# Attention and gated MLP in one program: the odd pair sums of attention's last unit go to VectorE, and the third accumulating DMA is issued behind pair 5 instead of pair 4

## The reference

```python
h = _layernorm(x, axis=-1) * (1 + ca) + sa
x = x + ga * _L0_attn_ref(h, Wq, Wk, Wv, Wo, bo)
h = _layernorm(x, axis=-1) * (1 + cb) + sb
x = x + gb * _L0_ffn_ref(h, w_gate, w_up, w_down)
```

```python
att = jnp.einsum('bhgqd,bhkd->bhgqk', q, k) / scale
att = jax.nn.softmax(att, axis=-1)
y = jnp.einsum('bhgqk,bhkd->bhgqd', att, v)
y = y.transpose(0, 3, 1, 2, 4).reshape(b, t, e)
return y @ Wo.T + bo
```

## Time and profile before

| | before |
|---|---|
| median of 3 runs | 3463.37 us (3461.37 to 3470.88) |
| profiled execution, span from the first to the last instruction | 3460.0 us |
| TensorE busy (matmuls) | 3409.4 us, 99% |
| VectorE, ScalarE, GpSimd busy | 65%, 46%, 47% |
| mean granted clock of TensorE | 0.995 |
| attention, last unit's end | 1988 us |

### The profile page before, as it was taken

One profiled execution on the slowest core, in us unless ns is written; L12 is line 12 of the kernel. 1 busy time (PEld: TensorE's weight loads), 2 busy tenths in 40 slices (PEclk: granted clock), 3 DMA queues, 4 the chain that ended last, 5 costly groups with the idle time before them and its releaser, 6 DMA issues.

```text
span 3460.0 us, 45394 instructions
## 1 busy us (share of the span) xinstructions
PE 3409.4 (99%) x17032; PEld 2290.5 (66%) x17032; DVE 2248.4 (65%) x3760; ACT 1597.7 (46%) x3008; POOL 1635.8 (47%) x728
## 2 busy tenths in 40 slices
PE   7999999999999999999999999999999999999999
PEld 5787455555555555555555378888888888887787
DVE  6766777777777777777777288644444444443727
ACT  3211666666666666666666623222222222224544
POOL 1223788988988998898898810000000000001000
PEclk9999999999999999999999999999999999999999
DMA  6666655556565555555545545611111111013212
GB/s 238 198 202 210 159 103 115 117 109 125 104 126 109 110 120 114 117 114 116 116 104 120 135 151 183 175 31 30 30 30 30 30 30 30 24 43 128 96 63 89
DMA packets 197444, 369.96 MB, mean 107 GB/s; under 512 B 44240, under 2 KB 119504, under 8 KB 178832
## 3 DMA queue, kind: packets, MB, share of 16 engines
q0 software_dynamic: 39712, 203.97, 25.7%
q1 hardware_dynamic: 154096, 157.31, 16.2%
q10 hardware_dynamic: 3456, 6.29, 0.6%
HBM read 167.90 MB, written 64.87 MB: 67 GB/s over the span
## 4 chain that ended last, share of the span: by engine, by line
PE 92%; DVE 3%; DMA 2%; ACT 1%; issue 1%; POOL 0%; SPq 0%; ACTq 0%; DVEq 0%; POOLq 0%
PE att_scores L1107 16%; PE att_scores_T L1121 14%; PE att_y_acc L1132 14%; PE gu_gate_acc L1712 13%; PE gu_up_acc L1712 13%; PE wo_acc L1405 5%; PE down_acc L2035 5%; PE down_acc L2060 5%; PE qkv_qk_acc L629 3%; PE att_den_acc L822 2%; DMA qkv_wqkv_raw<-in_wmod 1%; ACT qkv_h_affine L346 1%; DMA qkv_wmod_lo<-in_wmod 1%; PE qkv_v_acc L610 1%; DVE qkv_wmod L462 1%
## 5 line engine op out<-in xcount | busy, mean ns | idle before, releaser
L1040 DVE TENSOR_REDUCE att_chunk_max<-att_scores 128x1 f32<-128x512 f32 x1984 | 1213.0, 683 | 345.9 <-PE att_scores L1107 345.8
L1011 ACT ACTIVATE att_exp<-att_scores_T 128x512 f32<-128x512 f32 x2048 | 1049.9, 620 | 444.1 <-PE att_scores_T L1121 422.5
L950 POOL TENSOR_TENSOR att_exp_pair<-att_exp 128x2048 f32<-128x2048 f32 x256 | 1200.0, 4737 | 44.4 <-ACT att_exp L1011 44.0
L1132 PE MATMUL att_y_acc<-att_exp,att_v_head 128*32 128x512 f32 x4096 | 495.7, 602 | 0.0
L1569 POOL DMA_DIRECT2D inter_scratch<-gu_inter x84 | 45.2, 538 | 854.0 <-DVE gu_inter L1446 854.0
L1107 PE MATMUL att_scores<-att_kq,att_q_stack 96*128 96x512 f32 x768 | 327.4, 430 | 1.0 <-DVEq L1086 0.7
L1107 PE MATMUL att_scores<-att_k_stack,att_q_stack 96*128 96x512 f32 x768 | 325.0, 426 | 0.4
L1121 PE MATMUL att_scores_T<-att_q_stack,att_k_stack 98*128 98x512 f32 x768 | 299.1, 412 | 2.7 <-ACT att_exp L1011 2.3
L1121 PE MATMUL att_scores_T<-att_q_stack,att_kq 98*128 98x512 f32 x768 | 296.4, 405 | 0.7 <-ACT att_exp L1011 0.7
L1634 ACT ACTIVATE gu_magnitude<-gu_value 128x512 f32<-128x512 f32 (+1 forms) x88 | 55.7, 633 | 512.0 <-DVE gu_value L1670 512.0
L1669 DVE TENSOR_TENSOR gu_rounded<-gu_up_acc,gu_rounded 128x512 f32<-128x512 f32 x84 | 58.1, 692 | 312.2 <-PE gu_up_acc L1712 312.1
(11 more groups left out here) (245 smaller groups left out, 6093.0 us busy)
## 6 DMA issues: line engine op xcount, KB each, us to landing
att_exp_pair<-att_exp_pair POOLq DMA_DIRECT2D x128, 1024.0 KB, 7.3
att_q_stack<-q_scratch SPq DMA_DIRECT2D x72, 256.0 KB, 5.6
qkv_wqkv_raw<-in_wmod POOLq DMA_DIRECT2D x32, 512.0 KB, 4.6
shared_raw<-in_wd_t POOLq DMA_DIRECT2D x34, 256.0 KB, 2.9
qkv_x_tile<-in_x SPq DMA_DIRECT2D x16, 512.0 KB, 4.0
q_scratch<-qkv_qk_out_hi POOLq DMA_DIRECT2D x32, 256.0 KB, 3.6
q_scratch<-qkv_qk_out_lo POOLq DMA_DIRECT2D x32, 256.0 KB, 4.2
y_scratch<-att_y_out SPq DMA_DIRECT2D x32, 256.0 KB, 2.9
```

The lines of the kernel that those rows point to most:

```text
L950: nc.gpsimd.tensor_tensor(ps[PAIR_SLOT[j]][:], pr[2 * j % NP][:], pr[(2 * j + 1) % NP][:], ALU.add).then_inc(pair_done, 1)
L1011: nc.scalar.activation(pr[k % NP][:, h * NB:(h + 1) * NB], stp[bank_of(u, c, GH * k + h)][:], ACT.Exp, scale=INV_SQRT_DH).then_inc(exp_don ...
L1040: nc.vector.reduce_max(cmax[c % 2][:, q:q + 1], turn_buffer(u, c, q)[:], AX.X).then_inc(sm_done, steps_done(u, q))
L1132: ins = nc.tensor.matmul(yp[h * DH:(h + 1) * DH, :], vg[c // QB % 2][:, k, :], pr[k % NP][:, h * NB:(h + 1) * NB], start=(k == 0), stop=(k ...
```

## The change

In all units D2 is issued behind pair 5 instead of behind pair 4. In the last unit alone, pairs 1, 3, 5 and 7 are summed by VectorE (semaphore `last_pairs`), and pairs 0, 2, 4 and 6 stay on GpSimd; waits for a pair go through `wait_pair`, which knows both semaphores. VectorE takes pairs 1 and 3 ahead of the reciprocal of the unit before (`recip`), pair 5 behind it, then splits the first y tile, then takes pair 7, then splits the second y tile.

```diff
-    DMA_AFTER = {1: 0, 3: 1, 4: 2, 7: 3}
+    DMA_AFTER = {1: 0, 3: 1, 5: 2, 7: 3}
...
+        def wait_pair(eng, u, j):
+
+            if u < 0 or u < NU - 1:
+                eng.wait_ge(pair_done, NP // 2 + u * PAIRS + j + 1)
+            else:
+                eng.wait_ge(pair_done, NP // 2 + u * PAIRS + j // 2 + 1)
+                if j:
+                    eng.wait_ge(last_pairs, (j + 1) // 2)
...
+        def pair_inputs(eng, u, j):
+
+            eng.wait_ge(exp_done, NST + 2 * GH * (j + 1) + u * NX)
...
+            elif j == 5:
+                eng.wait_ge(dma_sum[0], 16 + u * 16)
...
             def sum_by_dma(u, i):
                 into, other = DMA_SUM[i]
-                pool.wait_ge(pair_done, NP // 2 + SUM_PAIRS[i] + 1 + u * PAIRS)
+                wait_pair(pool, u, SUM_PAIRS[i])
...
                 for j in range(PAIRS):
-                    pair(u, j)
+                    if u < NU - 1 or j % 2 == 0:
+                        pair(u, j)
...
-                            act.wait_ge(pair_done, k // 2 + 1 + u * PAIRS)
+                            wait_pair(act, *((u, k // 2 - NP // 2) if k >= NP else (u - 1, k // 2 + PAIRS - NP // 2)))
...
+            def last_pair(j):
+                pair_inputs(v, NU - 1, j)
+                nc.vector.tensor_tensor(ps[PAIR_SLOT[j]][:], pr[2 * j % NP][:], pr[(2 * j + 1) % NP][:],
+                                        ALU.add).then_inc(last_pairs, 1)
+
             for u in range(NU - 1):
                 unit(u, u % BODY, u // QB)
+            for j in (1, 3):
+                last_pair(j)
             recip(NU - 2)
+            last_pair(5)
             first_y()
+            last_pair(7)
             wo.lo_of_y(v, 1)
```

More of the change, by code:

```diff
@@ L721, in stage_attention @@
         pv_done, pair_done, den_done = sem("pv_done"), sem("pair_done"), sem("den_done")
-        quad_done = sem("quad_sum_done")
+        quad_done, last_pairs = sem("quad_sum_done"), sem("last_odd_pairs_done")
         dma_sum = [sem(f"dma_sum_done{i}") for i in range(len(DMA_SUM))]
@@ L796, in beyond @@
             return isinstance(u, int) and u + n >= NU
-        first_y_room = pair_done, NP // 2 + (NU - 1) * PAIRS + 5
-        second_y_room = pair_done, NP // 2 + (NU - 1) * PAIRS + 6
+        def wait_pair(eng, u, j):
[5 more added lines that the diff above has]
+                    eng.wait_ge(last_pairs, (j + 1) // 2)
         WO_HI_AT = range(2, 2 + FT)
@@ L808, in store_y @@
                          ).then_inc(y_stored, 16)
+        def pair_inputs(eng, u, j):
+            eng.wait_ge(exp_done, NST + 2 * GH * (j + 1) + u * NX)
+            if j == 0:
+                eng.wait_ge(den_done, 1 + u * ND)
+            elif j == 1:
+                if u:
+                    eng.wait_ge(quad_done, u)
+            elif j == 2:
+                if u:
+                    eng.wait_ge(dma_sum[3], u * 16)
+            elif j == 3:
+                eng.wait_ge(den_done, 3 + u * ND)
+            elif j == 4:
+                eng.wait_ge(den_done, 2 + u * ND)
+            elif j == 5:
+                eng.wait_ge(dma_sum[0], 16 + u * 16)
+            elif j == 6:
+                eng.wait_ge(dma_sum[1], 16 + u * 16)
+            elif j == 7:
+                eng.wait_ge(dma_sum[2], 16 + u * 16)
         def denominators(pe, u, i):
@@ L875, in den_trip @@
                     sp.wait_ge(y_stored, 16 + 16 * u)
-                    sp.wait_ge(*first_y_room)
+                    wait_pair(sp, NU - 1, 4)
                     sp.wait_ge(pv_done, NP + (u + 1) * KT + KT // 2 + 2)
@@ L929, in pair @@
             def pair(u, j):
[L930 to L949, removed]
+                pair_inputs(pool, u, j)
                 nc.gpsimd.tensor_tensor(ps[PAIR_SLOT[j]][:], pr[2 * j % NP][:], pr[(2 * j + 1) % NP][:],
@@ L961, in quad_sum @@
             def quad_sum(u):
-                pool.wait_ge(pair_done, NP // 2 + 6 + u * PAIRS)
+                wait_pair(pool, u, QUAD_AFTER)
                 nc.gpsimd.tensor_tensor(ps[4][:], ps[4][:], ps[1][:], ALU.add).then_inc(quad_done, 1)
@@ L1029, in _ @@
             nc.scalar.copy(wo.y_first[:], wo.yraw[0].rearrange("p k t -> p (k t)")).then_inc(wo.y_copied, 1)
-            act.wait_ge(*second_y_room)
+            wait_pair(act, NU - 1, 5)
             act.wait_ge(pv_done, NP + (NU - 1) * KT + KT // 2 + 4)
@@ L1063, in first_y @@
                 v.wait_ge(wo.y_copied, 1)
-                v.wait_ge(*first_y_room)
+                wait_pair(v, NU - 1, 4)
                 v.wait_ge(pv_done, NP + (NU - 1) * KT + KT // 2 + 2)
```

## The result

| | before | after |
|---|---|---|
| median of 5 runs, us | 3464.1 (3461.4 to 3470.9) | 3518.6 (3510.3 to 3523.5) |
| span of the profiled execution, us | 3460.0 | 3516.9 |
| ratio after to before | | 1.0155 [1.0143, 1.0166] |

The change costs 54.5 us, 1.6%. The forecast was 3492, 28.5 us of loss. The direction and the place were right; the size was half of what came.

The account below looks back on a forecast made before the run. TensorE was taken to set the pace. Span 3460.0 + 25.5 for held stores + 3 for scatter + 0 for the last unit = 3488.5 us; the median lies 3.4 us higher, so 3492 us, range 3474 to 3504.

Parts of the forecast that it names:

- Edit 1, the wait that goes: D2 behind pair 5 ends GpSimd's wait for D1, about 3.1 us a unit, for which TensorE does not pay.
- D2's issue: On GpSimd, D2 is issued 0.3 us behind pair 5's end, at 1522.8 instead of 1519.05, 3.7 us later.
- The held stores: Maxima's small stores wait for D2, land 7.1 to 7.5 us behind its issue, and delay next unit's first scores_T; chance 0.78.
- the rival "no change": At passages between units, the stores interleave with D2 or their descriptors are taken up first; time 3463, chance 0.12.
- the usual hold: TensorE starts each next unit 0.85 us later because of the maxima's stores, at 30 passages: 25.5 us.
- scatter, "0.1 us a unit": Accumulating DMAs' excess over their fastest landing reaches TensorE: 0.1 us a unit, 3 us in all, 0 to 0.4 possible.
- clock: Nothing counted; as a rival, each 0.85 us stop at a passage brings a 1.2 GHz stretch, 45 us more, 3537; chance 0.06.
- last unit: VectorE's four pairs in the last unit change the time by 0, with -1 to +2 us.
- The granted clock stays at 2.4 GHz there: Expected sign in the changed profile: no fall of the clock at the first scores_T of the units.
- 0.8 to 1.0 us longer: Expected sign in the changed profile: each unit lengthens by this much, all of it at the first scores_T.
- Edit 2: VectorE's four pairs in the last unit take 2.5 to 7.1 us each, hidden from TensorE; 0 for the whole.
- The 3.4 us that the forecast put between span and median: Added to the whole kernel's forecast span of 3488.5 us, because the median of runs lay 3.4 us above the profiled span.

Follow-up runs that it names:

- e1: The kernel before with only D2 moved behind pair 5 in all units, GpSimd keeping all pairs of the last unit; 3516.6 us, ratio 1.0147.
- e2: The kernel after with D2 back behind pair 4, the last unit's odd pairs still on VectorE; 3464.3 us, ratio 1.0002.
- e3: The kernel after with D2 cut in two: 1024 of 2048 columns behind pair 5, the other 1024 behind the quad sum; 3468.1 us, ratio 1.0010.
- e4: The kernel after with D2 cut in two: 1792 of 2048 columns behind pair 5, 256 behind the quad sum; 3488.9 us, ratio 1.0069.

## Why the prediction was wrong in size

**Edit 1, the wait that goes.** Right. It is gone, GpSimd waits for ScalarE instead, and nothing came of it.

**D2's issue.** Nearly right. I put 0.3 us between pair 5 and the issue, by the usual bracket. The row at 1566.44 has no bracket and starts 4.51 us behind pair 5's start, so D2 is some 0.4 us earlier than forecast. The bracket belongs to DMAs that wait for the pair sum just ahead of them, as D0, D1 and D3 do. D2 does not wait for pair 5: it adds the results of D0 and D1, its wait is for pair 3 (`SUM_PAIRS = (1, 3, 3, 7)`), and all its waits are long over. At all 31 D2s of units 0 to 30 the issue starts 0.05 to 0.08 us before pair 5's recorded end.

**The held stores.** Right as a mechanism (e1 against e2, e3 against e4, and the pieces in the records). They land 7.6 us behind D2's issue, against 7.1 to 7.5 forecast. The Trainium skill's rule on arbitration, cited ahead of the result from "DMA: Bandwidth & Descriptors", section "Queues, rings and completion order", agrees with these traces in its second half, that a packet is drained before the switch: the 8 KB pieces of D2, 128 in all or eight for each of 16 engines, had started by 6.3 us (but for one at each of two passages), and no piece of a store started before 6.43. That is what the trace shows of it; where one packet ends it does not show. Its first half, the turns between queues, gave the rival "no change", which is dead: all 31 stores were held, their fastest landing 3.3 us.

**The terms of the sum**, forecast and measured in units 0 to 30:

| term | forecast, us | measured, us |
|---|---|---|
| the usual hold | 30 x 0.85 = 25.5 | 31 x 0.57 = 17.7 |
| scatter, "0.1 us a unit" | 3 | 14.6 |
| clock | 0 | 17.9 |
| last unit | 0 | 0 (e2) |

The measured hold is the mean of the 19 usual passages, 10.9 / 19 = 0.57, on all 31 (0.52 without the last passage); the 14.6 is what is left of the 32.3. So the stops together came near the forecast's 28.5, but by two errors against each other: the usual hold was over-sized by 8 us (D2 was issued 0.4 us earlier than forecast, which the hold's 7.6 us in place of 7.5 took back in small part), and the scatter was under-sized by 12. **The scatter is the first step that failed.** I read its size from how accumulating DMAs scatter, and bounded it at 0.4 us a unit, which is their median less their minimum; it came to 0.47. A median does not see the few long ones. The 128 landings of that very trace average 7.5 us, 0.6 above the fastest. And the one stop of the kernel before was such a case: the store of the earlier trace rows took 3.31 us and landed 9.35 us behind its D2, which was issued at 1826.91, with an instruction packet 7.19 us behind that. I took from this row only the 0.04 us behind the landing. In the kernel after, D2's own landings average 7.42 us over the 31 passages, 0.46 above the fastest, as much as the term came to.

**The clock is the step that cost the result.** I had it as a rival in which each stop of 0.85 us brings a stretch or none does, and gave it 0.06. With all stops equal that would be a fair question. But the stops are not equal: the usual ones brought no stretch, and 8 of the 12 long ones did. What I set against the rival, that the work around a passage is dense, did not keep the clock up. By the distance from one scores_T to the next across the passage (0.24 us where nothing stops), a stretch came at 8 of the 11 passages with 1.6 to 3.2 us, and at none of the 20 with 1.2 or less; in e1 it was 9 of 11. In e4 it was 5 of 8 with 1.4 to 2.5 us. Why one stop brings it and an equal one does not is left open. The size of a stretch in the rival was about right, 1.5 us forecast and 17.9 / 8 = 2.2 measured; its number was wrong. It hung on the first error: had the scatter been given as a few long stops and not as a mean of 0.1 us, would have had to be asked for them. "The granted clock stays at 2.4 GHz there", a mark of the forecast, failed, as did "0.8 to 1.0 us longer" (49.0 / 31 = 1.6 us).

**Edit 2.** Right at 0. VectorE's four pairs (min/median/max ns) and the split behind them:

```profile
L1103 DVE TENSOR_TENSOR att_exp_pair<-att_exp x4: 2291/2606/3031, 2007.8 to 2046.5; 128x2048 f32<-128x2048 f32 x4
```

```profile
2046.49 3.03 DVE L1103 TENSOR_TENSOR att_exp_pair<-att_exp 128x2048 f32<-128x2048 f32 x1
2049.45 5.60 DVE L1243 TENSOR_TENSOR shared_split<-shared_raw,shared_split 128x1024 fp32r<-128x1024 f32 x1
```

A pair on VectorE takes 2.3 to 3.0 us: two ran with no sum of GpSimd beside them and took 2.29, a little under the 2.5 to 7.1 forecast, and two overlapped one and took 2.92 and 3.03. The split, usually 1.22 us, took 5.60 beside a pair sum of GpSimd, and ended at 2055.1, 1.1 us behind that sum's end (2047.33 + 6.63 = 2053.96). TensorE begins on its tile at about 2059, half-way through its 23.4 us block from 2046.63, so it was hidden by 4 us, as forecast.

**The chance part.** Some of the 54.5 us between the medians may be the start-up and the last unit, which move by several us from one execution to the next. In the profiled pair they are +8.7 and -2.1, and nothing was made of them. The 3.4 us that the forecast put between span and median is 1.7 here (3518.6 against 3516.9), and each run's time lies 1.7 to 2.2 us above its span; the rest was the one execution before, which lay under its median.

## What to carry to other kernels

Here a 1 MB accumulating DMA held every small store that was issued 3 to 5 us behind it (those issued 5.5 us and more behind it, as before the change, mostly landed in their usual 1.9 us). So before such a transfer is moved, look up which small store or load the next stage of the pacing engine waits for; cutting the transfer so that only a half stands in front took the cost away here. When a stall is estimated, forecast its spread and not its mean, and ask of the longest ones whether TensorE's clock falls behind them. In the profile after, such a loss shows as busy time, so compare matmul durations and the granted clock as well as the waits.

## What the runs showed of the hardware that was not expected

- Instruction-fetch packets appear to be held by an accumulating DMA as well, and to go ahead of small stores issued before they start: 12 of 31 passages, 0.3 to 2.3 us more each (a coincidence in the records, not isolated by a run).
- Distances of 1.6 to 3.2 us between two scores_T in dense work, 1.2 to 2.8 us of them idle, were followed by a stretch at 1.2 GHz in 8 of 11 cases in the kernel after and in 9 of 11 in e1; in e4 one with 0.98 us idle was. The distances of 1.2 us and less brought none, and filling the stops with 8 matmuls kept the clock at 2.4 GHz.
- SyncE's issue of the second store takes 1.38 us while D2 flows, 0.59 where only a half stands in front.
- GpSimd issues a DMA 0.3 us behind the pair sum ahead of it where the DMA waits for that sum, and 0.05 to 0.08 us before the sum's recorded end where its waits are long over (31 of 31 D2s).
